# Four mixed expert slots at 13, 17, 21 and 25 in place of 18, 22, 26 and 30 in a one-core decoder layer

## What is computed

```python
xf = x.reshape(-1, D)                       # 2048 tokens, D = 256
scores = softmax(xf @ gate_w.T)             # E = 8 experts
_, idx = top_k(scores + gate_b, K)          # K = 2
w = take_along_axis(scores, idx, -1)
rw = zeros((T, E)).at[arange(T)[:, None], idx].add(w)
h = silu((einsum('td,edh->teh', xf, w1) + b1) * (einsum('td,edh->teh', xf, w3) + b3))
oe = einsum('teh,ehd->ted', h, w2) + b2     # hidden H = 352
y = einsum('te,ted->td', rw, oe)
return (y + shared_expert(xf)).reshape(shape)
```

## Time and profile before

| | us |
|---|---|
| median of 3 runs | 578.79 |
| lowest and highest | 577.95, 579.46 |
| the profiled execution | 578.62 |
| its span, first to last instruction | 576.8 |
| PE busy | 556.0 (96%) |
| DVE busy | 443.8 (77%) |
| ACT busy | 315.7 (55%) |
| POOL busy | 234.3 (41%) |

### The profile page before, as it was taken

The page is one execution under the profiler, slowest core; times in us unless marked ns, Lnnn a source line. Parts: engine busy times, 40 slices in busy tenths (PEclk is TensorE's granted clock), DMA queues, the critical chain, the costliest instruction groups (busy, mean ns, idle before and its releaser), DMA issues.

```text
span 576.8 us, 11336 instructions
## 1 busy us (share of the span) xinstructions
PE 556.0 (96%) x3584; PEld 419.3 (73%) x3584; DVE 443.8 (77%) x835; ACT 315.7 (55%) x969; POOL 234.3 (41%) x228
## 2 busy tenths in 40 slices
PE   8999999999999999999999999999999999999991
PEld 6546566788687878888789787878876776666660
DVE  3999999999977788957969669966878656666740
ACT  3623424358869798695994949843312234444220
POOL 1110110306581743657535483516335443444444
PEclk9989999999999999999999999999999999999996
DMA  8930003353723240523315114984357645454424
GB/s 304 348 105 2 1 1 111 109 187 123 278 91 131 87 134 1 198 72 114 132 36 198 60 38 161 290 283 174 94 103 153 100 62 70 54 65 61 64 27 47
DMA packets 57194, 67.37 MB, mean 117 GB/s; under 512 B 31112, under 2 KB 50032, under 8 KB 54640
## 3 DMA queue, kind: packets, MB, share of 16 engines
q1 hardware_dynamic: 48960, 55.91, 31.3%
q0 software_dynamic: 6784, 8.95, 9.4%
q10 hardware_dynamic: 1392, 1.79, 1.1%
HBM read 55.58 MB, written 15.25 MB: 123 GB/s over the span
## 4 chain that ended last, share of the span: by engine, by line
PE 69%; DVE 9%; DMA 9%; issue 7%; POOL 4%; ACT 2%; POOLq 0%; SPq 0%; DVEq 0%
PE pb L737 9%; PE pb L638 6%; DMA out_dram<-R 6%; PE pb L501 6%; PE pb L603 6%; PE pb L551 6%; PE pb L567 5%; PE pb L771 5%; PE pb L442 4%; PE pb L518 4%; PE pb L650 4%; DVE R L1129 3%; PE pb L615 2%; PE pb L487 2%; DMA out_dram<-R,hidx 2%
## 5 line engine op out<-in xcount | busy, mean ns | idle before, releaser
L887 ACT ACTIVATE R<-R,mx 128x154 f32<-128x154 f32 x256 | 104.4, 415 | 0.1
L1745 POOL DMA_INDIRECT out_dram<-R x36 | 56.1, 1558 | 76.5 <-DMA out_dram<-R 51.0
L737 PE MATMUL pb<-R 128*128 x256 | 81.5, 461 | 0.0
L1005 ACT ACTIVATE R<-R 128x352 f32<-128x352 f32 x36 | 17.9, 496 | 98.3 <-DVE R L1570 76.2
L737 PEld LDWEIGHTS pb<-R 128*128 128x128 f32 x256 | 48.0, 189 | 23.9 <-issue 2.0
L501 PE MATMUL pb<-xnT,wq 128*128 128x256 f32 x256 | 58.2, 383 | 0.0
L878 ACT ACTIVATE R<-pb,bq 128x256 f32<-128x256 f32 x64 | 30.0, 473 | 47.7 <-PE pb L501 47.6
L501 PEld LDWEIGHTS pb<-xnT,wq 128*128 128x128 f32 x256 | 47.7, 190 | 7.8 <-issue 1.2
L1669 POOL DMA_INDIRECT xs_dram<-xn,pos x32 | 32.1, 1004 | 47.8 <-DVE pos L1313 39.5
L899 ACT COPY R<-pb 128x512 f32<-128x512 f32 x80 | 40.8, 616 | 18.4 <-PE pb L551 18.3
L1644 POOL TENSOR_TENSOR sd<-mv,cst 128x4 f32<-128x4 f32 x12 | 9.8, 814 | 97.7 <-DVE mv L1077 97.6
(11 more groups left out here) (199 smaller groups left out, 1144.7 us busy)
## 6 DMA issues: line engine op xcount, KB each, us to landing
R<-in_fside_dram SPq DMA_DIRECT2D x16, 1232.0 KB, 5.5
R<-in_L_ffn_w_dram SPq DMA_DIRECT2D x16, 352.0 KB
R<-in_mask_dram SPq DMA_DIRECT2D x16, 308.0 KB, 2.9
R<-xs_dram SPq DMA_DIRECT2D x128, 32.0 KB
KV<-in_ebias_dram SPq DMA_DIRECT2D x2, 1056.0 KB
out_dram<-x SPq DMA_DIRECT2D x4, 512.0 KB
R<-in_L_ffn_w_dram SPq DMA_DIRECT2D x8, 256.0 KB
x<-in_x_dram SPq DMA_DIRECT2D x3, 512.0 KB, 10.8
```

The lines of the kernel that those rows point to most:

```text
L737: ins = e.matmul(pb[:, u.i, 0:F], xsT[:, s % 2, k, :, :].rearrange("p r b -> p (r b)"), ew13[:, bass.ds(w_reg[s] * 1408 + q * 704 + k * F, ...
L887: ins = e.activation(att[t % 3][:, h, :], att[t % 3][:, h, :], ACT.Exp, bias=mx[:, a4, 1, h:h + 1], accum_out=mx[:, a4, 2, h:h + 1])
L1745: e.indirect_dma_start(out=out, out_offset=bass.IndirectOffsetOnAxis(ap=to.bitcast(U32), axis=0), in_=rows, in_offset=None, compute_op=ALU ...
```

## The change

The tuple `MIXED` gets four other numbers, and all that is worked out from it follows: the list `FULL`, which turns the first late slot from 16 to 18, the numbers of the adds, `pace`, and the slots in which ACT copies the weights. SP's waits for the scatters, the pads and the halves' table, which stood ahead of read 16, stand ahead of read 13; the wait for the late table falls away, since the halves' is written after it. POOL's wait for `base_out3` stands ahead of the first half of slot 13.

```diff
-MIXED = (18, 22, 26, 30)
+MIXED = (13, 17, 21, 25)
@@ POOL, the adds
-                if s == FULL[NA]:
+                if s == MIXED[0]:
                     w.wait_ge(base_out3, 16)
@@ SP, the reads
-            for s in range(NR, NA):
+            for s in range(NR, MIXED[0]):
                 read(s)
                 if s == NR:
                     base(3, base_out3)
-            w.wait_ge(slots.sem, slots["late"])
             w.wait_ge(to_xs, 128 * NCH)
             w.wait_ge(pad_xs, 16 + 16 * NE)
             w.wait_ge(slots.sem, slots["halves"])
-            for s in range(NA, NS):
+            for s in range(MIXED[0], NS):
                 read(s)
```

## The result

| us | before | after |
|---|---|---|
| median of 22 runs each, taken together | 577.81 | 579.72 |
| lowest and highest | 576.95, 579.46 | 578.23, 582.61 |
| the profiled execution, and its span | 578.62, 576.8 | 578.95, 576.9 |
| PE busy | 556.0 | 556.6 |
| DVE busy | 443.8 | 442.7 |

The ratio after to before is 1.0037, with a 95% interval of 1.0024 to 1.0050: slower by 2.1 us. The forecast was 579.2, +0.4; the time lies inside the range, but in the case "slower by over 0.3%", which had 0.22, and not in the one with 0.66. The 22 times of after stand in two heaps: 14 from 578.23 to 580.29, and 8 from 581.27 to 582.61.

A forecast was written before the change was run, and what follows sets the result against it. The chain of scatter-adds on POOL was taken to set the end. Add 12 starting 0.6 later and -0.2 inside the chain gave +0.4, a median of 579.2 us; the range was 577.0 to 581.8.

The forecast's parts named there:

- slower by over 0.3%: Outcome case for the whole time, more than 1.7 us slower than before: chance 0.22.
- What bounds: Scatter-adds on POOL, mostly waiting for earlier adds from add 14 (481.80) to the last (572.17), set the end, not PE.
- The waits that are moved: SP's waits moved ahead of read 13, POOL's base-row wait to add 13: cost nothing.
- Where add 12 starts: Add 12 on POOL starts at 474.4, 0.6 later than before; bounds 474.1 and 474.9.
- Inside the chain: Add 12 to the end takes 98.2 against 98.36 before: the move is worth -0.2 us.
- mixed pairs: Adds of the four mixed slots, from first half to the next slot's add: 30.06 in sum, unchanged by the move.
- serial steps: Adds waiting until their predecessor has landed: 4.74 each, eleven after add 12 making 52.2; two more than before.
- free or PE-paced: Adds following their own expert's previous tile: seven of 1.92 (13.4) and a last one of 2.5 to 2.6.
- The first mixed read too late: SP's first mixed read takes 10.4, add 12 starts at 476.7, 2.3 beyond forecast: 581.5; chance 0.18.
- The halves filling idle time for nothing: The two added serial steps do not bind, the end comes 5.6 earlier, 573.6; chance 0.07.
- PE taking over: Late reads stall PE by over 6 us in total and the end follows PE: at most forecast plus 1; chance 0.05.
- the forecast's case: The central forecast of +0.4, 579.2 us: chance 0.65, its spread reaching past +1.7 a little.

The follow-up runs named there:

- The added wait on the chain: Changed kernel with the free add of slot 27 made to wait for its predecessor: 582.25 us, 1.0072 to the kernel before.
- the one before it: Changed kernel with the add of slot 7 made to wait for its predecessor: 578.40 us, 1.0016 to the kernel before.
- the two late cuts: Kernel before with mixed slots at 18, 23, 27 and 31 instead of 18, 22, 26 and 30: 583.71 us, 1.0093.
- the one with the waits moved: Kernel before, mixed slots unmoved, with only SP's and POOL's waits placed as in the change: 577.67 us, 0.9991.
- the one with more traffic: Kernel before with ACT issuing a 16 KB DRAM to DRAM copy in each slot from 18 on, 19 in all: 577.32 us, 1.0013.
- the later read: Changed kernel with five more register loads on SP ahead of read 13: 582.41 us, 1.0070 to the kernel before.
- 13, 19, 23, 27: Changed kernel with mixed slots at these places instead of 13, 17, 21, 25: 576.22 us, 0.9966 to before; measured again 575.78, 0.9968.
- SP relieved: Mixed slots at 13, 19, 23, 27, with ACT issuing each mixed slot's `hidx` fetch and chunk 3's base rows instead of SP: 573.25 us, 0.9943 to before.
- 15, 19, 23, 27: Changed kernel with mixed slots at these places instead of 13, 17, 21, 25, cutting no run: 577.62 us, 0.9998 to before.

## Why the prediction was right or wrong

**What bounds.** Right, but for where it begins. The added wait on the chain cost 2.0 to 2.4 (the one before it nothing), the two late cuts cost 5.4 to 6.0 against 5.6, and in all 14 traces the last add starts 3.2 us or more after its result could have been handed over. I let the chain begin at add 12 to 14; but adds 17 and 21 of before still waited for results. The sum was not hurt, since it took them as steps of that kind.

**The waits that are moved.** Right: 0.9991 for them alone.

**Where add 12 starts.** Right in size, partly by another way. Forecast 0.6 later, of which 0.29 for PE's mixed slot. Add 9 to add 12 took 12.48 to 12.84 in four traces with the mixed slots of the change, and 11.98 in all four of before: 0.5 to 0.9 more. I had the delay at turn 14, at 467.4 to 468.4, because I counted the mixed read as a burden for the next read. Turn 14 came at 465.84, with 0.35 of waiting: read 13 started 1.26 earlier than I had it (454.42 for 455.68; all of this trace is 0.96 earlier at add 9), and turn 14 was 3.7 behind the start of its read and not 4.6. It was the mixed slot's own turn that was late, by 1.72, since it needs all 11 of its DMAs; I had not given that wait a price. Of the 0.5 to 0.9, PE's mixed slot is 0.3 (12.28 and 12.29 where turn 13 waits under 0.8), and the late turn 13 the rest, 0.2 to 0.6. Only a much later read counts in full: 3.3 more at turn 13 gave 3.4 more at add 12.

**Inside the chain.** This is where the forecast of -0.2 failed, and the term that moved most against it is that of the mixed pairs, 30.06, "the same halves in the same order". The sums by kind of step, add 12 to 35, from four traces of before (the two of the kernel, the one with the waits moved and the one with more traffic) and five of after (the two of the kernel, the later read, and the two added waits; add 27 of the fifth is counted with the 1.87 that it takes without its added wait), mean with lowest and highest:

| us | forecast after | before | after |
|---|---|---|---|
| serial steps, 9 and 11 | 52.2 | 41.9 (41.4 to 42.7) | 51.6 (51.2 to 52.4) |
| mixed pairs, 4 | 30.06 | 30.3 (29.5 to 31.6) | 31.4 (29.5 to 32.6) |
| free or PE-paced, 10 and 8 | 15.9 | 25.6 (25.5 to 25.7) | 16.2 (16.0 to 16.8) |
| add 12 to 35 | 98.2 | 97.9 (96.8 to 99.2) | 99.2 (97.9 to 100.4) |

The exchange that the whole prediction turned on came out nearly even, as summed: two more serial steps cost 9.6, and the adds that PE paced give back 9.4, of which adds 13 and 14 are 8.0 and the other eight, with 17 and 21 among them, 1.4. The mixed pairs cost 1.1 more than before in the mean, where I had them equal. With 0.7 for add 12 that is 2.0, and the runs show 2.1. But the 1.1 is not shown beyond the scatter: four of the five traces lie at 31.2 to 32.6, the fifth at 29.5, and the four of before at 29.5 to 31.6. Why the pairs should be dearer stays open too; the last section has what goes with it. The serial steps were lighter than the 4.74 that I took (4.69), which hid part of the miss against the forecast, but not against before, since theirs are lighter as well. I had one trace and took its steps for fixed; among the four of before it is the one with the highest sum of serial steps.

**The rivals.** The first mixed read too late: its mechanism is there, at some 0.4 us in place of 2.3. The halves filling idle time for nothing: no; but with one cut fewer they do gain, 2 us. PE taking over: never; the nearest to it is add 15, which waited 0.3 to 1.0 for its result.

**The chances.** With a spread of 1.5 us between two traces of one kernel, more of the forecast's case should have reached past +1.7: a central value of +0.4 with 0.66 within 0.3% was too sure.

## What to carry to other kernels

Count what a reordering does to the chain that sets the end by kinds of step, and look for the place where an item costs nothing: an expensive item moved into another engine's idle time pays, as long as it does not break a run of cheap ones; 13, 19, 23, 27 won 2 us where 13, 17, 21, 25 lost 2. An item that needs many DMAs is late by its own time in the issuing queue: look whether anything waits for it, and if so issue it further ahead (here waits of turn 13 of up to 2.4 us cost at most 0.6, one of 5.0 cost 2 more). Take the length of a step from more than one execution where a difference of 0.3% is to be called.

## What the runs showed of the hardware

The longest steps of the chain all have a fetch of instructions beside them. The trace shows single packets on the queues q8 (16 KB) and q14 (8 KB) of kind "instruction". In the changed kernel, the DMA queues between adds 21 and 21b (516.29 to 521.01; packets, MB, share of 16 engines):

```profile
q1 hardware_dynamic: 855, 0.16, 22.7%
q0 software_dynamic: 80, 0.07, 14.7%
q8 instruction: 1, 0.02, 1.9%
```

and between 13 and 13b (478.47 to 482.00), which took 3.53:

```profile
q1 hardware_dynamic: 681, 0.12, 23.5%
q0 software_dynamic: 80, 0.07, 19.2%
```

The longest step of any is that from add 26 to 27 in the second trace of 13, 19, 23, 27, first POOL and then its queues from one start to the other:

```profile
534.94 1.89 POOL L1745 DMA_INDIRECT out_dram<-R  x1 [0.30 <-issue]
541.78 1.43 POOL L1745 DMA_INDIRECT out_dram<-R  x1 [4.95 <-DMA out_dram<-R]
```

```profile
q0 software_dynamic: 288, 0.26, 34.3%
q1 hardware_dynamic: 1412, 0.26, 21.9%
q8 instruction: 1, 0.02, 0.9%
q14 instruction: 1, 0.01, 0.3%
```

Over the 14 traces I sorted the steps from 470 us on that end at least 0.25 after the result was there by whether such a packet falls between 0.8 after one start and 0.7 ahead of the next:

| us | without a fetch | with one |
|---|---|---|
| serial | 104 steps, 4.41 to 5.08 | 43 steps, 4.49 to 6.84 |
| to the second half | 38 steps, 3.28 to 3.65 | 18 steps, 3.37 to 4.88 |
| behind a mixed slot | 44 steps, 3.78 to 4.16 | 12 steps, 3.86 to 5.24 |

Every step longer than the longest without a fetch, 21 of them, holds one; 52 of the 73 steps with a fetch are not longer. With the slots of the change (five traces) they fall on 21b (4.72, 4.88, 4.88), 18 (4.55, 4.61, 4.82), 25b (3.78, 3.96, 4.40) and 26 (4.42), all in four of the traces; the fifth has only add 33 (5.50). With those of before (four) they fall on 22b (3.84, 4.18, 4.40) and 27 (4.23, 5.24), and one trace has none. In the two traces of 13, 19, 23, 27 it is add 27 (5.72 and 6.84), but with SP relieved there is none; in 15, 19, 23, 27 it is add 17 (6.40), in 18, 23, 27, 31 adds 27b (3.67) and 32 (4.36). So they tend to come back at the same adds of a kernel, and not in every execution. That would explain why the mixed pairs of this change are dearer in four traces of five, and perhaps the two heaps of its times. It is a correlation: no run moved a fetch, and the one that was to imitate it did not make long packets. The Trainium skill has the DMAs of all engines interleave on the same 16 DMA engines (DMA: Bandwidth & Descriptors, "Issuing engines are not separate DMA queues"); a long packet ahead of an add's short ones would fit that, and no run here shows it.

Also not expected: a contiguous copy of 16 KB from DRAM to DRAM went out in 16 packets of 1 KB. And a register load on SP is not small. In the kernel with the later read the mixed read starts 4.00 after the last DMA of read 12, in the changed one 454.42 - 453.17 = 1.25 after it, so the five loads took 2.75, 0.55 each (an estimate, from two traces); SP's rows in the two kernels, that with the loads first:

```profile
455.17 0.35 SPq L1878 DMA_DIRECT2D R<-xs_dram  x1
459.17 1.88 SPq L1865 DMA_DIRECT2D R<-xs_dram  x4
```

```profile
453.17 0.35 SPq L1878 DMA_DIRECT2D R<-xs_dram  x1
```
